# Moving one residual store and the layer-norm steps at the start of a feed-forward

## The reference

```python
def _layernorm(x, axis=-1, eps=1e-05):
    m = jnp.mean(x, axis=axis, keepdims=True)
    v = jnp.var(x, axis=axis, keepdims=True)
    return (x - m) / jnp.sqrt(v + eps)
...
x = x + _L0_attn_ref(_layernorm(x), ...)     # 16 heads, causal
x = x + _L0_ffn_ref(_layernorm(x), ...)      # 32 experts, the 8 best of each token
x = x + _L1_attn_ref(_layernorm(x), ...)     # gated state-space scan, then w_out
x = x + _L1_ffn_ref(_layernorm(x), ...)      # silu(x @ gate) * (x @ up) @ down, 1376 wide
```

## Time and profile before

| | |
|---|---|
| time of three runs, us | 2416.76, 2417.96, 2418.59; median 2417.96 |
| the profiled execution | 2418.59 us; its span 2416.7 us |
| busy, share of the span | PE 94%, DVE 61%, POOL 45%, ACT 40% |
| slice 604 to 665 us (the attention block's end and dispatch), PE | 5 tenths busy |
| slices after 2054 us (the feed-forward), PE | 9 tenths or more, the last 8 |
| granted clock of PE, mean | 0.968 |

### The profile page before, as it was taken

One profiled execution on the slowest core, in us unless ns is written; L12 is line 12 of the kernel. 1 busy time (PEld: TensorE's weight loads), 2 busy tenths in 40 slices (PEclk: granted clock), 3 DMA queues, 4 the chain that ended last, 5 costly groups with the idle time before them and its releaser, 6 DMA issues. The chain is left out here.

```text
span 2416.7 us, 45610 instructions
## 1 busy us (share of the span) xinstructions
PE 2267.6 (94%) x12486; PEld 1740.7 (72%) x12488; DVE 1467.2 (61%) x3409; ACT 978.1 (40%) x2194; POOL 1096.2 (45%) x981
## 2 busy tenths in 40 slices
PE   7989999998589999999998699999899999999998
PEld 5865555556378899889897388887656666888886
DVE  6446666757755555555554559997066668555554
ACT  3125666655444444444443432222365554212121
POOL 3118888887266666666676211112276663000000
PEclk9989999999799999999999699999999999999999
DMA  5469999989789999999997435456597841000001
GB/s 183 126 171 343 348 354 362 355 324 369 274 222 285 277 279 251 268 280 267 267 227 122 156 120 183 159 183 207 146 254 183 202 105 40 27 27 13 26 10 70
DMA packets 256769, 487.11 MB, mean 202 GB/s; under 512 B 32573, under 2 KB 149717, under 8 KB 246902
## 3 DMA queue, kind: packets, MB, share of 16 engines
q1 hardware_dynamic: 188582, 267.61, 35.8%
q0 software_dynamic: 62976, 212.42, 31.3%
q10 hardware_dynamic: 5088, 5.56, 0.7%
HBM read 588.73 MB, written 198.66 MB: 326 GB/s over the span
## 5 line engine op out<-in xcount | busy, mean ns | idle before, releaser
L1578 PE MATMUL m_ps_u<-m_ring,m_xT_hi 128*128 x1280 | 369.3, 349 | 0.2 <-DVE m_xT_lo L1690 0.2
L1546 POOL DMA_INDIRECT expert_sum<-x_res,token_of x160 | 255.1, 1595 | 175.4 <-DMA expert_sum<-x_res,token_of 75.1
L1578 PEld LDWEIGHTS m_ps_u<-m_ring,m_xT_hi 128*128 128x128 f32 x1280 | 235.8, 189 | 0.9 <-issue 0.6
L779 ACT ACTIVATE probs<-ps_c 128x512 f32<-128x512 f32 (+3 forms) x384 | 176.9, 491 | 136.3 <-PE ps_c L690 91.9
L1578 PE MATMUL m_ps_u<-m_ring,m_xT_lo 128*128 x640 | 216.4, 338 | 0.0
L1539 POOL DMA_INDIRECT m_xg<-x_rows,token_of x160 | 173.2, 1083 | 85.0 <-issue 77.1
L2045 PE MATMUL s_ps<-s_x_hi,s_w_hi 128*128 128x512 f32 x512 | 200.0, 391 | 2.7 <-POOL s_w_lo L2006 2.7
L2045 PE MATMUL s_ps<-s_x_hi,s_w_lo 128*128 128x512 f32 x512 | 199.2, 389 | 0.0
L2045 PE MATMUL s_ps<-s_x_lo,s_w_hi 128*128 128x512 f32 x512 | 199.2, 389 | 0.0
L2842 DVE TENSOR_TENSOR x_res<-f_ps_o,x_res 128x512 f32<-128x512 f32 x176 | 109.3, 684 | 143.6 <-PE f_ps_o L2730 143.6
L1704 DVE SCALAR_TENSOR_TENSOR m_h<-m_silu,m_xg,m_ps_u 128x128 f32<-128x128 f32 x160 | 55.7, 348 | 230.9 <-ACT m_silu L1643 230.9
(11 more groups left out here) (369 smaller groups left out, 5645.3 us busy)
## 6 DMA issues: line engine op xcount, KB each, us to landing
m_ring<-w_split SPq DMA_DIRECT2D x160, 1536.0 KB
m_ring<-w_split SPq DMA_DIRECT2D x160, 768.0 KB
w_split<-e_gu_parts POOLq DMA_DIRECT2D x32, 1536.0 KB, 7.8
proj<-s_out SPq DMA_DIRECT2D x32, 1024.0 KB, 4.0
e_raw_gu<-w_experts POOLq DMA_DIRECT2D x32, 768.0 KB, 10.3
w_split<-e_dn_parts POOLq DMA_DIRECT2D x32, 768.0 KB, 8.0
e_raw_dn<-w_experts POOLq DMA_DIRECT2D x32, 512.0 KB, 9.4
q_st<-q_parts SPq DMA_DIRECT2D x32, 256.0 KB, 6.5
```

Of the source, the lines that this page charges most:

```text
L779: nc.scalar.activation(probs[a][j % RING][:, :width], ps_c[(j * BATCH + a) % BUFS][:, :width], ACT.Exp, scale=SCALE).then_inc(exp_done, 1)
L1546: pool.indirect_dma_start(acc[j % 2], rows_at(j), y[j % TURNS], None, bounds_check=PADDED - 1, oob_is_err=True, compute_op=ALU.add).then_i ...
L1578: last = nc.tensor.matmul(ps_u[b % 2][:, :W_UP], x[b % 2][:, k, :], ring[:, first + k * GU_ROW:][:, bass.ds(place, W_UP)], start=(n == 0), ...
```

## The change

In the first place the store of `x_res` to `acc[0]` moves behind the wait for the cleared buffer and behind the store of the padding rows; its wait for `added` goes. In the second place `TURNED_BEHIND` goes from 3 to 2; on ACT each group's square roots move from ahead of the previous group's silu to the head of their own round; on DVE the moments of groups 2 and 3 and the scales and normalization of groups 2 and 3 move into the rounds, so that a round is: scales and normalize of the next group (from round 1 on), moments of the one after, low parts of the next group, hidden product, low part of h.

```diff
@@ project_and_route, sync @@
                 sp.wait_ge(xn_ready, i + 1)
                 sp.dma_start(x_rows[toks(of_tile(i)), :D], xn[:, i, :]).then_inc(rows_stored, 16)
-            sp.wait_ge(added, TILES)
-            sp.dma_start(acc[0][:N_TOK, :].rearrange("(n p) d -> p n d", p=P), x_res[:, :, :]).then_inc(acc_ready, 16)
             sp.wait_ge(zeroed, 1)
             sp.dma_start(x_rows[N_TOK:, :], zeros[:, :ROW_W]).then_inc(pads_ready, 16)
+            sp.dma_start(acc[0][:N_TOK, :].rearrange("(n p) d -> p n d", p=P), x_res[:, :, :]).then_inc(acc_ready, 16)
             sp.dma_start(acc[0][N_TOK:, :], zeros[:, :D]).then_inc(acc_ready, 16)
@@ lut_feed_forward @@
-        AHEAD, TURNED_BEHIND = 3, 3
+        AHEAD, TURNED_BEHIND = 3, 2
@@ scalar @@
             for i in tiles_of(0):
                 high_x(i)
-            deviations(1)
             for r in range(AHEAD):
+                deviations(r + 1)
                 for i in tiles_of(r + 1):
                     high_x(i)
-                if r + 2 < GROUPS:
-                    deviations(r + 2)
                 silu_of(0, r)
@@ vector @@
             moments(1)
             scanned.add_last[0](dve)
-            moments(2)
             for i in tiles_of(0):
                 low_x(i)
             scales(1)
             for i in tiles_of(1):
                 normalize(i)
             scanned.add_last[1](dve)
-            dve.wait_ge(scanned.o_added, scanned.added_until + 2)
-            moments(GROUPS - 1)
             for r in range(AHEAD):
+                if r > 0:
+                    scales(r + 1)
+                    for i in tiles_of(r + 1):
+                        normalize(i)
+                if r + 2 < GROUPS:
+                    moments(r + 2)
                 for i in tiles_of(r + 1):
                     low_x(i)
-                if r + 2 < GROUPS:
-                    scales(r + 2)
-                    for i in tiles_of(r + 2):
-                        normalize(i)
                 hidden(0, r)
                 if r < 2:
                     low_h(0, r)
```

## The result

The changed kernel took 2433.09 us (median of 5 runs, 2429.18 to 2442.3), beside 2418.59 for the kernel before (2416.76 to 2424.5). The ratio is 1.0055, 95% interval 1.0031 to 1.008: slower by 13.3 us (7.5 to 19.3). The sign was forecast with 0.73; the time lies 3.1 us above the range. The profiled execution took 2427.61 us, its span 2425.8.

What follows compares the result with a forecast made beforehand. TensorE, busy 94%, bounds the feed-forward's start; a queue bounds the attention block's end. Feed-forward +6.0, store 0, later expert weights +0.5 make +6.5 on 2418.59, 2425.1; the median, 0.6 lower, is 2424.5 us, range 2419 to 2430.

Steps and rivals of the forecast that it cites:

- The sign: Whole kernel: slower by over 0.2% (above 2422.8 us), chance 0.73.
- The feed-forward's start: From the scan to the first down product: reordering makes TensorE wait, 6.0 us later, bounds 4.5 and 9.
- the moved part: Feed-forward's start: output-projection part behind the turns adds 1.75 us; with the old wait gone, group 1 starts 0.95 later.
- +1.9: Before group 2's turns: TensorE waits for VectorE's late normalized tiles, losing 1.9 us.
- +2.2: Before group 2's product: low parts stand behind group 3's moments on VectorE, costing TensorE 2.2 us.
- the old stall: Kernel before: TensorE's 0.65 us wait before the second token group, for VectorE's low parts of x; predicted to go.
- The root's chain: Before group 2's turns: ACT's root waits behind high part of h and table load (1.28), delaying normalized tiles to 2052.1.
- The table switch: ACT's square roots: 1.28 us per load by the trace; the page's price adds 1.38 per switch, 8.8 instead of 6.0.
- The clock: TensorE, 2049 to 2063: clock falls after waits, about 1.6 us each; with dearer table switches, 2426.5 to 2430, chance 0.18.
- the third stall: Before group 3's turns: TensorE waits for late normalized tiles, so the second product starts 0.9 us later.
- The store: Attention block's end: boundary 2.65 us earlier, given back behind bulk traffic; 0 at the dispatch's end, bounds -2.65 and +2.
- SP's stall behind the 4 MB: Block boundary: even 3 us of stalled issues would be covered by SP's later wait; no chance of its own.

Runs made afterwards that it cites:

- the reordering alone: Kernel before with square roots, scales, normalization and moments reordered on ACT and DVE, TURNED_BEHIND staying 3; timed +9.9 us, then +1.9 us when repeated.
- the three pieces alone: Kernel before with all edits of the feed-forward's start (TURNED_BEHIND 2, reordered ACT and DVE steps), residual store left in place; timed +13.8 us, then +3.9 us.
- the roots put back: Changed kernel with ACT's square roots put back ahead of its silu, VectorE's order staying changed; timed +5.3 us against the kernel before.
- the ruler: Kernel before with eight extra copies of group 1's low parts on VectorE, a stall of known size on TensorE's path; timed +8.2 us, then +7.7 us.

## Why the prediction was right or wrong

**The feed-forward's start: right, term by term.** Predicted +0.95 net for the moved part, +1.9, +2.2, +0.9, sum 6.0. Measured in the traces without a clock fall: 1.94, 2.25, 0.82, and 0.8 left for the moved part net of the old stall; sum 5.8. The moved part bought nothing, its cover being the wait for the tile: from the fourth turn to the end of group 0's gate product it is 1.73 us more (11.83 before, 13.56 in the second trace of the changed kernel), predicted 1.75. The root's chain was right too: taking the root out of it freed 0.9 us, as expected. The loops behind gave nothing back.

**The table switch: the trace's price held.** Load 1.28 at 2051.27, root at 2052.56, with no drain between. The Trainium skill ("ScalarE: Activation LUTs", section "What ACT_TABLE_LOAD costs") gives 2.66 for load and drain together; the measured stalls leave no room for it here.

**The clock, a rival with part of 0.18: it happens, in some executions.** Eight traces have TensorE's stall of 1.96 to 1.98 us before group 2's product with nothing filled in. In three of them the clock fell behind it: one of three of the changed kernel, both of the reordering alone, none of the two of the three pieces alone, and not in the one with the roots put back. With the ruler's stall filled it stayed away, in one trace. Its price was 1.6 us for the product in the changed kernel, but that covered the third stall with its 0.8, so some 0.7 net; 1.4 to 2.35 in the ruler. My 1.6 a fall was the right size, its frequency was unknown. What I had set against it, that TensorE would be busier than in the stretch of the earlier trace rows, did not decide: the fall stands in one trace of the changed kernel and not in the others, which have the same stalls.

**The store: a part of its mechanism right, its terms mis-sized.** I had the memset 3.1 earlier, since `w_split` would land sooner and TensorE's last turn would be the gate. In the first trace it came 3.6 earlier behind the last row store, over all traces 1.3 (standard error 1.1): the wait of the earlier trace rows was a frequent case and not the rule, and with the store moved TensorE was the gate in three traces of six. I had given SP's stall behind the 4 MB no chance of its own. It came in all six traces; with the moved issue's own 0.44 and somewhat slower issues of the zeros it makes 4.2 us from memset to dispatch, so that the boundary comes 2.9 us later (standard error 1.0) and not 2.65 sooner. The table's load came 5.4 later in the first trace, counted from the last row store (predicted 5.5), and 7.3 over all traces. It cost nothing, since SP's spare time took it, falling from 5.6 to 2.3; but SP did not become the last engine, as I had written: in all six traces it still waited 1.9 to 2.8 us for TensorE. The dispatch's end therefore moved with the boundary, by some 3 us, where I had 0. What I gave 0.5 us, the collision of the expert weights with the first gathers, costs 2.1. In all the first up product is 5.1 us later (standard error 1.1) where the sum had 0.5.

How much of this reaches the time is not shown. The experts' stage behind it is 3.2 shorter (standard error 2.2), so that its end lies 1.9 later (standard error 2.3), and the timed run of the store alone says -2.4 (-7.3 to 2.2). In that stage the DMA engines are busy 97% of the time, and TensorE 99%; which of the two takes the delay up, no run isolates.

The Trainium skill ("DMA: Bandwidth & Descriptors", section "Queues, rings and completion order") says that each DMA engine takes the descriptors of one ring in ring order. It also says that a later one may finish its write before an earlier one, so my "can't pass" went further than the page. The traces agree with the order: with the 4 MB moved, the table's load came 8.6 us behind the table's stores, with them last 14.6, in the old place 4.1. They don't prove it, since the issues of the table's stores slowed as well (2.93 and 6.18 us for three, 1.27 before).

**The step that failed is the last one of the sum,** where I put "the profiled execution's own 2418.59" and "the median of the runs is 0.6 below" under the prediction and let the range hold the unknown costs of the change only. Three runs within 1.9 us made the base look sharp. It was not: over 134 more runs the kernel before has a mean of 2424.1, 5.5 above the base that I took, with medians of 2421 to 2426, and the experts' stage alone scatters by 5 us. The changed kernel was steadier in its level, with medians of 2433.09, 2431.52 and 2429.9. On a base of 2424.1 the same +6.5 makes 2430.6, where 2433.09 was measured.

This is not all of it. In the first comparison the kernel before came to 2418.59 again, so there the miss stands wholly in the difference, 14.5 against 6.5. With a standard deviation of 6 us for one run, a median of five has a standard error of some 3 us, and the difference of two such medians an interval of some 9 us either side (my estimates from these runs); the repetitions gave +7.8 and +12.6 for the same pair of kernels. So that first difference was in part a draw, and the term of the change was short as well (next paragraph). A range for the median of five runs needed some 5 us for the scatter beside the bounds of the terms, on both sides; 2433.09 would have been inside. My statement that 0.2% can be told from no change was a little too fine: the intervals reach 0.18 to 0.27% to either side with 12 runs against 29 or 35, and 0.25% in the first comparison.

**What stays open.** The changed kernel costs +11.0 (7.6 to 14.4) by three measurements. The traces show 5.8, or 6.5 with the clock's fall, plus 0 to 5 us for the store; the first trace has 7.6, since a second blocked tile adds 1.06, which comes without the change too. My 6.5 is below the interval, so the sum is probably short by 1 us or more, and the cause of that remainder stays open. Whether the store makes it can't be told: alone it measured -2.4, and the pieces alone, without the store, measured +9.7 (5.5 to 13.8), which holds 5.8 only at its edge. The ruler speaks against a hidden second price for stalls. No version here is measurably faster than the kernel before.

## What to carry to other kernels

Work placed ahead of a wait is free as long as the wait outlasts it; moved behind, it costs its full length. Each operation put in front of the one that a busy TensorE waits for costs its own length and can be summed from rows. Before giving a range, ask how far the stages that the change does not touch scatter: one profile and three runs that agree are one draw, not the level. And a large store in a queue also holds up what is issued behind it, the small table on the critical path included.

## What the runs showed of the hardware

- An issue on SP's queue stalls while a 4.19 MB store stands ahead of it: a 256 KB store took 4.41 to 4.65 us to issue in six traces, and 1.13 to 1.26 in eleven with the large store issued 10 us or more earlier. With the large store last, three small stores took 6.18 us to issue in place of 1.27.
- VectorE's 128x512 tensor_scalar took about 1.5 to 1.6 us in place of 0.545 while POOL ran a tensor_tensor on 128x512, in all 18 traces; a start of POOL 0.02 us sooner made it two tiles instead of one.
- TensorE's granted clock went to the lower of its two levels (1.2 of 2.4 GHz) behind a stall of 5.56 us in two traces of two, and not in the one trace in which 4.9 us of matmuls stood in the stall. Behind a stall of 1.96 us it fell in some executions of one kernel and not in others (the changed kernel: one of three).
- Over all timed runs, 0.001 less of mean granted clock goes with 2.0 us more of time (standard error 0.16, kernels taken out). This is a correlation; no run shows which causes which.
- ACT's table load took 1.28 us in every trace, and the next activation started 0.01 us behind it where its input was there.
- The experts' stage, with the DMA engines at 0.97 and TensorE busy 0.99, scattered by 5.2 us (standard deviation) over 18 traces; the feed-forward, with the DMA engines at 0.09, by 0.3.
